# A four-stage transformer block on one core: one mask matmul per score bank, the row turn after the second copy, and VectorE's loop branch in another place

## The reference, cut to what matters

```python
x = x + _L0_attn_ref(_layernorm(x), ...)   # linear attention: q @ (k.T @ v), no softmax
x = x + _L0_ffn_ref(_layernorm(x), ...)    # 8 routed experts (top 2) and a shared one, width 128
x = x + _L1_attn_ref(_layernorm(x), ...)   # 16 heads of 8, causal softmax over 512 tokens
x = x + _L1_ffn_ref(_layernorm(x), ...)    # 16 experts, each takes its best 512 tokens

# _L1_attn_ref
att = jnp.einsum('bqhd,bkhd->bhqk', q, k) * SCALE
att = jnp.where(mask[None, None, :, :], -jnp.inf, att)     # the mask comes to j > i
att = jax.nn.softmax(att, axis=-1)
out = jnp.einsum('bhqk,bkhd->bqhd', att, v).reshape(B, T, C)

# _L1_ffn_ref: what each expert reads
xn = xf / rms * norm_weight
logits = xn @ router_weight.T + router_bias
_, idx = jax.lax.top_k(logits.T, top_k)                    # over all 8192 tokens
```

## Time and profile before

| what | value |
|---|---|
| median of 3 runs (lowest, highest) | 1889.29 us (1885.23, 1890.84) |
| the profiled execution, its own time | 1888.15 us |
| its span, first to last instruction | 1885.8 us |
| mean granted TensorE clock | 0.907 |
| TensorE matmuls busy | 1558.1 us (83%) |
| VectorE busy | 1217.5 us (65%) |
| ScalarE busy | 862.5 us (46%) |
| GpSimd busy | 518.3 us (27%) |

### The profile page before, as it was taken

How to read it: one execution, slowest core, us unless ns; L and a number is a source line. 1 busy time by engine, 2 the same in 40 slices (tenths; PEclk the granted TensorE clock), 3 DMA queues, 4 the chain that set the end, 5 groups by cost and what they waited for, 6 DMA issues and landing times.

```text
span 1885.8 us, 35247 instructions
## 1 busy us (share of the span) xinstructions
PE 1558.1 (83%) x10840; PEld 974.4 (52%) x10840; DVE 1217.5 (65%) x3591; ACT 862.5 (46%) x1787; POOL 518.3 (27%) x498
## 2 busy tenths in 40 slices
PE   2889989999999999998989898999998821356765
PEld 2455656565655555565656565656564411244654
DVE  5567868686868686867777686868675358821110
ACT  1436464645555554545464646464553412423331
POOL 1322222131313131312222222213121020038886
PEclk7879999999999999999999999999999765578897
DMA  2031121303030303031221212130303000034443
GB/s 70 1 79 47 40 64 29 73 18 85 7 84 7 84 15 81 24 67 39 52 54 37 54 37 58 33 77 14 79 8 84 8 12 0 1 73 95 91 85 60
DMA packets 83244, 90.77 MB, mean 48 GB/s; under 512 B 19520, under 2 KB 73024, under 8 KB 78528
## 3 DMA queue, kind: packets, MB, share of 16 engines
q1 hardware_dynamic: 71872, 80.76, 17.5%
q0 software_dynamic: 11264, 8.92, 3.5%
HBM read 58.95 MB, written 29.92 MB: 47 GB/s over the span
## 4 chain that ended last, share of the span: by engine, by line
PE 52%; DVE 18%; issue 15%; POOL 6%; DMA 3%; ACT 3%; SPq 1%; DVEq 1%; POOLq 0%; ACTq 0%
PE fa L675 7%; PE ba L585 6%; PE ba L580 6%; PE fa L667 6%; PE bo L834 5%; PE fa L685 4%; POOL out L552 3%; PE ba L587 2%; PE facc L685 2%; PE ba L953 2%; DVE passed L1488 2%; PE ba L582 2%; DVE nm L1258 2%; DMA QT<-nmT 2%; POOL got L522 2%
## 5 line engine op out<-in xcount | busy, mean ns | idle before, releaser
L1013 ACT ACTIVATE probs<-ba 128x512 f32<-128x512 f32 x640 | 352.3, 598 | 191.9 <-PE ba L582 190.7
L458 POOL TENSOR_TENSOR x<-x,gd 128x512 f32<-128x512 f32 x144 | 182.5, 1267 | 615.4 <-ACT gd L991 598.1
L580 PE MATMUL ba<-QT,KT 75*128 75x512 bf16 (+3 forms) x1024 | 262.2, 319 | 27.7 <-ACT probs L1013 14.5
L585 PE MATMUL ba<-KT,QT 72*128 72x512 bf16 (+3 forms) x1024 | 244.2, 305 | 7.4 <-DVE nm L1258 3.2
L580 PEld LDWEIGHTS ba<-QT,KT 75*128 75x128 bf16 x1024 | 106.7, 104 | 188.0 <-ACT probs L1013 104.1
L582 PE MATMUL ba<-mask_k,identb 128*128 128x128 bf16 x1024 | 200.2, 229 | 0.0
L1258 DVE TENSOR_REDUCE nm<-ba 128x1 f32<-128x512 f32 x256 | 174.3, 681 | 36.0 <-PE ba L587 36.0
L587 PE MATMUL ba<-mask_q,identb 128*128 128x128 bf16 x1024 | 192.9, 222 | 0.0
L834 PE MATMUL bo<-probs,vp 128*32 128x512 f32 (+3 forms) x2048 | 182.2, 445 | 1.7 <-ACT probs L1013 0.9
L675 PE MATMUL fa<-f_nT,w 128*128 128x512 f32 x320 | 174.3, 627 | 2.5 <-DVE hh L1250 1.5
L667 PE MATMUL fa<-f_nT,w 128*128 128x512 f32 x320 | 173.8, 625 | 0.0
(11 more groups left out here) (279 smaller groups left out, 2785.1 us busy)
## 6 DMA issues: line engine op xcount, KB each, us to landing
QT<-qk_parts SPq DMA_DIRECT2D x96, 192.0 KB
KT<-qk_parts SPq DMA_DIRECT2D x96, 192.0 KB
qk_parts<-qkp SPq DMA_DIRECT2D x32, 384.0 KB, 2.5
fc<-in_L_ffn_fc_weight SPq DMA_DIRECT2D x32, 256.0 KB, 3.1
xin<-in_L_attn_x SPq DMA_DIRECT2D x16, 256.0 KB, 7.8
qk_parts<-qkp SPq DMA_DIRECT2D x16, 256.0 KB, 2.7
out<-x SPq DMA_DIRECT2D x16, 256.0 KB, 2.3
xn_rows<-row SPq DMA_DIRECT2D x16, 256.0 KB, 6.6
```

The costliest lines, as they stand in the source:

```text
L458: pool.tensor_tensor(x1[:], x1[:], gd[:, e % 2], ALU.add).then_inc(S["s_x1g"], 1)
L580: pe.matmul(bank[:, col:col + w], lhsT=KT[0:K_ROWS, head, blk * P:(blk + 1) * P], rhs=QT[0:K_ROWS, head, blk * P:], start=True, stop=False)
L585: pe.matmul(bank[:, col:col + w], lhsT=QT[0:QK_ROWS, head, blk * P:(blk + 1) * P], rhs=KT[0:QK_ROWS, head, 0:w], start=True, stop=False)
L1013: act.activation(probs[:, pair % 3, f_], ba[n % 3][:], ACT.Exp, scale=SCALE).then_inc(S["s_exp"], 1)
```

## The change

Three edits, with the same arithmetic.

1. A score bank gets one mask matmul. Where it holds two diagonal blocks, the matmul writes both, as a two-block output with a step between the blocks, and reads the mask twice by a stride of zero. Only the bank's first score matmul has the flag `start`.
2. VectorE writes the rows of t ahead of its second copy of `bo`. TensorE turns them after fill 29, where it did so ahead of fill 25, and also runs `f_out` ahead of fill 29. ScalarE's copy `rowT` goes from behind exponential 26 to behind exponential 29.
3. VectorE's y phase is cut earlier: `norm(1)`, `f_x1`, `outputs(2)` and `t_logits` now stand behind the cut, with the loop branch ahead of them. One more pass is written out ahead of the loop, which starts at 2.

```diff
--- before.py
+++ after.py
@@ -574,17 +574,23 @@
                 groups = [(h, 2, 0), (h, 0, 384)] if not by_key else [(h, 1, 0), (h, 3, 384)]
             else:
                 groups = [(h, 1, 0), (h + 1, 1, 256)] if not by_key else [(h, 2, 0), (h + 1, 2, 256)]
+            diagonal = []
             for head, blk, col in groups:
+                first_ = not diagonal
                 if by_key:
                     w = SEQ - blk * P
                     pe.matmul(bank[:, col:col + w], lhsT=KT[0:K_ROWS, head, blk * P:(blk + 1) * P],
-                              rhs=QT[0:K_ROWS, head, blk * P:], start=True, stop=False)
-                    last = pe.matmul(bank[:, col:col + P], lhsT=identb[:], rhs=mask_k[:], start=False, stop=True)
+                              rhs=QT[0:K_ROWS, head, blk * P:], start=first_, stop=False)
+                    diagonal.append(col // P)
                 else:
                     w = (blk + 1) * P
                     pe.matmul(bank[:, col:col + w], lhsT=QT[0:QK_ROWS, head, blk * P:(blk + 1) * P],
-                              rhs=KT[0:QK_ROWS, head, 0:w], start=True, stop=False)
-                    last = pe.matmul(bank[:, col + w - P:col + w], lhsT=identb[:], rhs=mask_q[:], start=False, stop=True)
+                              rhs=KT[0:QK_ROWS, head, 0:w], start=first_, stop=False)
+                    diagonal.append((col + w) // P - 1)
+            n_, step_ = len(diagonal), max(diagonal[-1] - diagonal[0], 1)
+            blocks = bank[:].rearrange("p (n k) -> p n k", k=P)[:, diagonal[0]:diagonal[-1] + 1:step_]
+            mask = mask_k if by_key else mask_q
+            last = pe.matmul(blocks, lhsT=identb[:], rhs=mask[:, None, :].to_broadcast([P, n_, P]), start=False, stop=True)
             last.then_inc(S["s_st" if by_key else "s_S"], 1)
 
         def down_bank(e):
@@ -871,11 +877,12 @@
                 fills(20, 21)
                 outputs(1, 22, 23, 24)
                 if_f(f_kvo)
-                if_t(t_turn_row, r)
                 fills(25, 26, 27)
                 if_b(turn_outputs, 1)
-                fills(28, 29)
+                fills(28)
                 if_f(f_out)
+                fills(29)
+                if_t(t_turn_row, r)
                 fills(30, 31)
                 outputs(2, 32, 33, 34)
                 if_t(t_router)
@@ -1037,11 +1044,11 @@
                 exps(20, 24)
                 if f is not None:
                     copy(kvo[:], fa[1][:, 0:D], "s_kvo", f + 1, "s_kvoc")
-                exps(25, 26)
+                exps(25, 29)
                 if t is not None:
                     act.wait_ge(S["s_T4"], t + 1)
                     act.activation(rowT[:], facc[:], ACT.Copy, scale=norm_col[:]).then_inc(S["s_nT4"], 1)
-                exps(27, 36)
+                exps(30, 36)
                 if f is not None:
                     copy(f_nT[:], fa[0][:], "s_T2", f + 1, "s_nT2")
                 exps(37, 39)
@@ -1395,6 +1402,10 @@
 
                 if rest:
                     fc.b = f
+                    if_b(norm, 1)
+                    if_f(f_x1)
+                    if_b(outputs, 2)
+                    if_t(t_logits)
                     if_b(norm, 2)
                     if_f(f_logits)
                     if_f(f_gates)
@@ -1414,12 +1425,8 @@
                 if_b(norm, 0)
                 if_f(f_kvm)
                 if_t(t_square)
+                if_t(t_row)
                 if_b(outputs, 1)
-                if_t(t_row)
-                if_b(norm, 1)
-                if_f(f_x1)
-                if_b(outputs, 2)
-                if_t(t_logits)
 
             def y_whole(b, f, r, t):
                 y_phase(b, f, r, t)
@@ -1430,8 +1437,10 @@
             x_phase(0, None, None, 1)
             y_whole(None, 1, 0, None)
             x_phase(1, 0, None, 2)
-            y_phase(0, 2, 1, None)
-            with dve.Fori(1, BATCH - 2) as i:
+            y_whole(0, 2, 1, None)
+            x_phase(2, 1, 0, 3)
+            y_phase(1, 3, 2, 0)
+            with dve.Fori(2, BATCH - 2) as i:
                 y_phase(i - 1, i + 1, i, i - 2, True)
                 x_phase(i + 1, i, i - 1, i + 2)
                 y_phase(i, i + 2, i + 1, i - 1)
```

## The result

The changed kernel takes 1855.23 us (median of 4 runs, 1851.95 to 1857.81), the kernel before 1887.26 us (4 runs, 1884.49 to 1890.84): a ratio of 0.9824, with a 95% interval of 0.9806 to 0.9842. It gains 32 us where I forecast 59, and lies above my range of 1822 to 1850. Of the cases I had written down it is the rival "the branch turns into the new wait", to which I gave 0.07. Medians and intervals leave out one execution, in experiment 7 (2299.99 us), whose clock was far lower throughout, 0.634.

What follows compares the result with a forecast made beforehand. TensorE, busy 83% of the span, was taken as the bound, through its waits and slow clock; 23.9 + 20.2 + 5.8 + 6.5 + 2.6 = 59.0 us off the median of 1889.29 gave 1830, range 1822 to 1850.

Steps and rivals of the forecast that it cites:

- the branch turns into the new wait: Rival: VectorE's moved branch makes TensorE stand ahead of the third output group; 1842 to 1862 us, chance 0.07.
- Its cost of about 3.1 us stays and moves behind the copy: VectorE's loop branch keeps its cost at the new place, from 892.02 to near 895.1, with norm(1) done near 895.7.
- So it is hidden, with 0.9 us to spare: VectorE's norm(1) ends before TensorE wants it at 896.6, ahead of the third output group, so the moved branch costs nothing.
- The rows first, turn later: Rows of t ready before TensorE's later row turn: 23.9 us of waits, 20.2 of clock, 5.8 after the loop.
- the clock's part of that gain: Clock falls to 0.50 behind TensorE's waits for the rows disappear: 18.9 us plus 1.3 for the last pass, 20.2.
- After the loop: In the two y phases after the loop TensorE's third output group starts earlier: 2.9 us, twice, 5.8 us.
- The first turn of the x phase: TensorE's wait of 0.54 us for the last copy of bo goes, in 12 passes: 6.5 us.
- The masks: One mask matmul fewer in 768 places on TensorE, 5 ns each: 3.8 us, of which 2.6 counted.

Runs made afterwards that it cites:

- experiment 7: The kernel before with only the second edit (rows written ahead of the second copy and turned later): 1832.75 us, ratio 0.9694.
- experiment 2: The changed kernel with SyncE's QT and KT loads for the next sequence's first half of heads released after fill 32 instead of 20: 1817.35 us, ratio 0.9627.
- experiment 1: The changed kernel with VectorE's loop branch back in its old place behind the logits of t, loop starting at 1 again: 1822.84 us, ratio 0.9655.
- experiment 6: The kernel before with only the first edit, the single mask matmul: 1871.71 us, ratio 0.9903.
- experiment 5: The kernel before, branch in its old place, with SyncE's loads for the first half of the heads released there by the third output group: 1952.26 us.
- experiment 8: The kernel before with only the third edit, VectorE's branch ahead of norm(1), rows still behind the second copy: 1898.98 us, ratio 1.0045.
- experiments 3 and 10: The changed kernel with VectorE's passes written out without a branch: 1805.72 us; the same with the first half's loads released behind fill 32: 1803.92 us.

## Why the prediction was wrong

**The step that failed** is "Its cost of about 3.1 us stays and moves behind the copy: from 892.02 it ends near 895.1, and `norm(1)`, 0.6 us long, near 895.7", and with it "So it is hidden, with 0.9 us to spare". From the branch at 437.37 to the reciprocal it took 5.25 us, and 4.94 to 6.32 over the taken branches, not 3.1. I took the gap for a constant, on "the gap hardly varies". All twelve of its samples stood where no data moved. The place to which it went is one of the two busiest of the pass for the DMA engines: in the kernel before the share is 0.76 from 892.0 to 895.0, and 0.84 in the 3.4 us behind that, which my own row said. I read only the clock in it. The slack was smaller than I had it too. In experiment 2, with a gap of the old length, `norm(1)` ends at 519.5 and TensorE comes at 520.16, so 0.7 us is left and not 0.9.

**Its price.** Against experiment 2 the twelve passes are 1055.25 - 1015.52 = 39.7 us longer. Of these 25.1 are TensorE's waits for `norm(1)` inside the loop. The rest is TensorE itself, busy for 987.88 against 973.29, 14.6 longer, with a fall of the clock in 9 passes and none in experiment 2. The rival had the mechanism, its place and its price: 1842 to 1862.

**The rows first, turn later: right.** In experiment 1 TensorE waits for no `row` in the loop and the clock is 1.00. For this edit, its share after the loop included, I had 23.9 + 20.2 + 5.8 = 49.9 us, and experiment 7 gained 1890.54 - 1832.75 = 57.8. Where the other 8 us come from no trace shows. In the changed kernel the clock's part of that gain was mostly given back to the new wait.

**After the loop: right.** In the changed kernel the second group ends at 1401.92 and the third starts 3.1 us later; I had 3.4, against 6.3 before. In the other y phase after the loop it is 3.1 as well.

```profile
1401.49 0.43 PE L840 MATMUL bo<-probs,vp 128*32 128x128 f32 x8
1403.89 0.60 PE L735 MATMUL facc<-ident,row 128*128 128x128 f32 x4
1405.03 1.06 PE L840 MATMUL bo<-probs,vp 128*32 128x512 f32 x8
```

**The first turn of the x phase: half right.** Its wait of 0.54 is gone, and 0.42 of it is back in experiment 1, where the branch is back. But another wait grew, that of TensorE for the first copy of `bo` in the y phase:

```profile
341.06 0.66 PE L749 MATMUL bo<-ident,oT 128*128 128x128 f32 x4 [0.94 <-DVE oT L1384]
```

In experiment 1 the same row has 0.58:

```profile
341.30 0.65 PE L749 MATMUL bo<-ident,oT 128*128 128x128 f32 x4 [0.58 <-DVE oT L1384]
```

So 0.36 of a pass came back there, with the new layout of VectorE's code, and experiments 1 and 2 have the same pace (84.7 and 84.6). Of the 6.5 us forecast, 1016.16 - 1015.52 = 0.6 was left in the passes. In all twelve passes of the changed kernel and of experiment 2 VectorE has a gap of 0.30 to 0.32 between two small steps there, and an instruction packet starts some 0.6 us behind its end; what causes the gap stays open.

**The masks: too small.** A mask of two blocks takes 0.11 from start to start, as forecast:

```profile
437.97 0.27 PE L593 MATMUL ba<-mask_k,identb 128*128 128x256 bf16 x1
438.08 0.38 PE L582 MATMUL ba<-QT,KT 75*128 75x512 bf16 x1
```

The rule of the Trainium skill, "Advanced Engine Details and Errata", section "PSUM Cachelines", that a non-contiguous pattern slows a matmul significantly, is not borne out for blocks of 128 columns. The gain of about 0.9 us a pass, where I had 0.2, comes in part from what stands behind a mask. In the kernel before:

```profile
296.00 0.22 PE L587 MATMUL ba<-mask_q,identb 128*128 128x128 bf16 x1
296.06 1.07 PE L667 MATMUL fa<-f_nT,w 128*128 128x512 f32 x2
296.97 0.38 PE L585 MATMUL ba<-KT,QT 72*128 72x512 bf16 x1
```

and in experiment 1:

```profile
292.86 0.27 PE L593 MATMUL ba<-mask_q,identb 128*128 128x256 bf16 x1
292.97 1.02 PE L681 MATMUL fa<-f_nT,w 128*128 128x512 f32 x2
293.83 0.61 PE L725 MATMUL bo<-w_o,b_nT 128*128 128x128 f32 x4
```

The float32 pair takes 0.91 behind a mask of 128 columns and 0.86 behind one of 256, and so it is at nearly all such places of the x phase, also in experiment 6 with its old order. I had priced the mask and not its neighbour.

**In sum**, had the fetch cost what it cost before, the forecast of 1830 would have been 12.7 us too high (experiment 2). Most of it is the masks, by the 0.9 us a pass of experiment 6 where I had 0.2.

## What to carry to other kernels

The cost of a taken branch of VectorE was here that of a transfer. Before it is moved, look at the DMA share at the new place, not at the engine's order alone, and don't take a gap for constant when all its samples stand in a quiet stretch. A hand-set transfer can be moved out of the way by one constant, which here was worth more than the change itself. And a rival with a price on record is worth little if a row already quoted could have settled its chance.

## What the runs showed of the hardware

- A taken branch on VectorE costs 2.75 to 3.1 us with the DMA engines quiet and 4.82 to 6.35 beside loads of `QT` and `KT` at a share of 0.8 (the changed kernel and experiment 5; up to 7.6 from the branch on in experiment 8). The same loop's branch took 0.2 to 0.3 us on TensorE, ScalarE and GpSimd, with no packet of its own.
- Not all traffic counts alike, though which of its properties does is open. DRAM to DRAM transfers of 128 KB at a share of 0.5 left most gaps at 2.8; with 192 KB each they were 3.14 to 3.65.
- Releasing the half-0 transfers late cost nothing here, releasing them early 38 us in the changed kernel (experiment 2) and at most 2 us without the branch (experiments 3 and 10).
- A mask matmul with a repeated input and an output of two separate blocks of 128 float32 columns runs at the pace of 256 contiguous ones, 0.11 us.
- The fall of the clock follows most such waits and not all. Of the eleven behind taken branches in the changed kernel the two shortest, 1.48 and 1.60 us, leave it at 1.00; behind those of 1.79 us and more it is 0.50 for 3.4 us, though TensorE is busy throughout. No bound follows from that: a wait of 1.84 brought none in the first pass of the kernel before, nor did waits of 2.71 and 2.62 in experiment 8 (633.41 and 1179.53).

```profile
531.13 1.07 PE L840 MATMUL bo<-probs,vp 128*32 128x512 f32 x8 [1.60 <-DVE ao L1278]
...
1238.56 1.06 PE L840 MATMUL bo<-probs,vp 128*32 128x512 f32 x8 [1.48 <-DVE ao L1278]
```

These are the changed kernel's two waits for `norm(1)` in the loop that no fall followed.
